# Attention projections as three float16 products of split rows and weights, split on ScalarE and GpSimd

## The chip, the cores and the metric

The kernel runs on one core of a Trainium2 chip. The metric is the device time of one execution in microseconds, and the time stated for a kernel is the median of its runs. One execution of each kernel is recorded by the hardware profiler. In the profile TensorE is PE (its weight loads are PEld), VectorE is DVE, ScalarE is ACT, GpSimd is POOL and SyncE is SP, whose queue starts the DMAs.

## What is computed

The input `x` is 2 x 128 x 256 x 256 (batch, channels, height, width) in float32. Two layers follow, each added to its own input: a window attention and a 3 x 3 convolution, each over a group norm of 32 groups.

```python
x = x + _L0_conv_ref(_gn(x), W_qkv, W_out, rel_height, rel_width)
x = x + _L1_conv_ref(_gn(x), weight, bias)
...
qkv = jnp.einsum('bchw,oc->bohw', x, W_qkv)
q, k, v = jnp.split(qkv, 3, axis=1)
q = q.reshape(b, INNER, nW, WS, nW, WS).transpose(0, 2, 4, 3, 5, 1)
k = unfold_windows(k)
v = unfold_windows(v)
...
attn = jnp.einsum('bnd,bmd->bnm', q * SCALE, k)
attn = attn + rel_pos_emb(q, rel_height, rel_width) + FIXED_MASK
attn = jax.nn.softmax(attn, axis=-1)
out = jnp.einsum('bnm,bmd->bnd', attn, v)
...
return jnp.einsum('bchw,oc->bohw', out, W_out)
```

Windows are 8 x 8 positions for the queries and 12 x 12 for keys and values (two rows and columns of halo), with 4 heads of 32 channels. The mask lets a query see only those keys whose row and column have one parity each, so the work falls into four parts by the parity of row and column. All products of the attention have 128 channels or fewer on the contracted side.

## The kernel before

The program runs in three stages, one after the other. The first reads `x` once for the group norm's moments (`bn_stats`) and prepares the weights. The second, the attention, is the subject here. The third is the convolution, which has already its rows and weights split into a high and a low float16 part and computes three products (`th` by `wc_h`, `tl` by `wc_h`, `th` by `wc_l`).

**Units and groups.** The attention handles 128 units. A unit is a strip of 8 rows by 128 columns (half a row of the image; `h` is the half), with its halo. A unit has 16 windows, four groups `g` of four windows each, and its rows are kept by parity in `PAR = 4` planes of `PLANE = 396` columns (66 x 6). Group number `n = 4u + g`. Every engine has its own program, written out by hand as `body(u, s, slot, on)`, which is called for each unit `u` and contains all that the engine does in the time of that unit for several units at different depths of the pipeline; a loop of four such bodies runs over the middle units. The engines meet through counting semaphores (`need` and `wait_ge`). So the order within an engine is fixed by the text of its `body`, and an instruction that waits holds up all that stand behind it on that engine.

**TensorE** (lines 378 to 468), in each group: the scores of group n (`ps_s`, 16 products, L421), the first transposes of group n-3 (`ps_t`, L401), `project` (L386 the query product of 256 columns into `ps_q`, L389 the key product of 396 columns into `ps_k`) of one of the next unit's four pieces, the value products of group n-3 (L434: for each of the four planes, 108 columns of `zf` are the loaded operand and 128 columns of `wq` are streamed), the products with the probabilities of group n-4 (`ps_o`, L451), the second transposes of n-3 (L401), and the output product (L462), which shares the bank `ps_q` with the query product. A float32 product is two matmul instructions in the trace.

**VectorE** (lines 471 to 552): adds the output product to `x1` (L495), sums the relative logits (L502 to `brel`), sums the exponentials (L506), copies the relative logits out (L511), reciprocal (L517), adds `erel` to the scores (L521), and takes their maximum (L527). To this come, in g0, two `bn_stats` (L533), in g1 and g3 the four copies from `qf` into the block-diagonal `qb` (L541), and in g2 two reductions over tiles (L548). The scores of a unit's g0 wait for both `qb` copies of that unit.

**ScalarE** (lines 555 to 622): exponential of n-2 (L576), the copy of the first transposes to `pt` (L581), of the query (L562) and key (L566) products, of the values (L588), of the output of the heads (L593), of the second transposes (L599), and then a piece of the normalised rows `zf` of unit u+2: in g0 a one-column copy that carries a wait (L608) and the rows of one parity (L610), in g1 those of the other, in g2 the two halo rows (L616).

**GpSimd** (lines 625 to 662): `erel` (L635), the normalised probabilities `d` (L642), two products for the relative logits (L651), and the subtraction of the maximum (L658).

**SP** (lines 347 to 376): loads the rows `xb` of unit u+3, stores `x1`, and loads the rows that are added to it.

`zf` has four slots of four planes, `xb` two halves. `z_at` addresses a plane of a slot.

## Time and profile before

| | |
|---|---|
| Time, median of 3 runs | 4083.1 us (4082.2 to 4085.4) |
| The profiled execution | 4085.44 us, with a span of 4083.6 us |
| Matmuls (PE) busy | 3730.3 us, 91% of the span |
| VectorE (DVE) busy | 3414.0 us, 84% |
| ScalarE (ACT) busy | 2976.6 us, 73% |
| GpSimd (POOL) busy | 2257.8 us, 55% |
| Chain that ended last | `ps_c` L808, 25% of the span, which is the convolution stage |

The span runs from the first to the last instruction of the execution, and what lies around it is about 1.8 us. The page cuts the span into forty slices, and these show three parts: the first stage up to about 200 us, in which TensorE does nothing, the attention up to about 3020 us, and the convolution from about 3060 us to the end. In the attention every slice looks like the one before. A busy share is the share of time in which a record of the engine is open; consecutive records of one engine overlap by some 0.1 us, so that the distance from start to start is the better measure of what an instruction costs its engine, and from start to end of what it costs who waits for it. The chain of the page follows only what ended last, and since the stages are separated it stops at the convolution; the attention has to be read from its timeline and its waits.

### The profile page before, as it was taken

The numbers are of one execution on the slowest core, as the hardware profiler recorded it, in microseconds if no ns is written. First come the engines' busy times: TensorE is split into PE (matmuls) and PEld (weight loads), VectorE is DVE, ScalarE is ACT, GpSimd is POOL, SyncE is SP. The second block draws the span as 40 slices with busy tenths as digits, with TensorE's granted clock in tenths as the row PEclk, the third lists the DMA queues.
The fourth block names the chain that finished last, engine by engine and source line by source line (L and its number), as shares of the span: only waits on it lengthen the run. The fifth ranks groups of instructions, "written<-read, shape, count | busy, mean of one in ns | idle before, by whom it ended". The sixth has DMA issues, their size and how long they took to land. (4 is left out here: it accounts for less than half of the span.)

```text
span 4083.6 us, 130797 instructions
## 1 busy us (share of the span) xinstructions
PE 3730.3 (91%) x48644; PEld 2631.8 (64%) x48644; DVE 3414.0 (84%) x6126; ACT 2976.6 (73%) x5317; POOL 2257.8 (55%) x2824
## 2 busy tenths in 40 slices
PE   0089999999999999999999999999958999999999
PEld 0067777777777777777777777777743444444444
DVE  9868888888888888888888888888878888888887
ACT  0078778778778878878877878877737777777774
POOL 0045555555555555555555555555536666666664
PEclk9999999999999999999999999999979999999999
DMA  9723233333233233233233233233214333343332
GB/s 372 312 75 86 82 93 85 83 93 86 81 93 87 81 93 87 80 93 87 80 93 88 79 93 87 80 93 87 73 58 173 152 149 152 149 153 152 155 145 94
DMA packets 489933, 462.48 MB, mean 113 GB/s; under 512 B 9264, under 2 KB 468912, under 8 KB 469040
## 3 DMA queue, kind: packets, MB, share of 16 engines
q1 hardware_dynamic: 489520, 455.92, 34.6%
q8 instruction: 388, 6.36, 0.6%
q14 instruction: 25, 0.20, 0.0%
HBM read 321.40 MB, written 134.48 MB: 112 GB/s over the span
## 5 line engine op out<-in xcount | busy, mean ns | idle before, releaser
L635 POOL TENSOR_TENSOR sb_erel<-sb_brel 128x288 f32<-128x288 f32 x512 | 352.1, 688 | 871.3 <-DVE sb_brel L502 871.2
L900 POOL TENSOR_TENSOR sb_tf<-sb_cf 128x1024 f32<-128x1024 f32 x256 | 609.6, 2383 | 393.1 <-DVE sb_tl L882 371.1
L651 POOL TENSOR_TENSOR sb_prod<-sb_rel,sb_shift 128x192 f32<-128x192 f32 x1024 | 596.8, 603 | 199.8 <-DVE sb_rel L511 199.8
L421 PEld LDWEIGHTS ps_s<-sb_kf,sb_qb 128*64 128x64 f32 x16384 | 520.3, 138 | 254.7 <-issue 237.0
L401 PE MATMUL ps_t<-sb_ident,sb_d 128*108 128x128 f32 x4096 | 662.4, 284 | 1.0 <-ACT sb_pt L599 1.0
L541 DVE COPY sb_qb<-sb_qf 32x512 f32<-32x512 f32 x1024 | 635.8, 621 | 27.6 <-ACT sb_qf L562 16.3
L421 PE MATMUL ps_s<-sb_kf,sb_qb 128*64 128x54 f32 x16384 | 586.3, 225 | 76.3 <-DVE sb_qb L541 73.8
L808 PE MATMUL ps_c<-sb_th,sb_wc_h 128*128 128x512 f16 x1536 | 584.9, 381 | 39.9 <-DVE sb_tl L882 39.9
L434 PEld LDWEIGHTS ps_v<-sb_wq,sb_zf 128*108 128x108 f32 x4096 | 511.1, 173 | 153.0 <-issue 80.5
L808 PE MATMUL ps_c<-sb_th,sb_wc_l 128*128 128x512 f16 x1536 | 583.9, 380 | 0.0
L808 PE MATMUL ps_c<-sb_tl,sb_wc_h 128*128 128x512 f16 x1536 | 583.8, 380 | 0.0
L434 PE MATMUL ps_v<-sb_wq,sb_zf 128*108 128x128 f32 x4096 | 530.4, 272 | 0.0
L642 POOL TENSOR_TENSOR sb_d<-sb_scores,sb_srcp 128x288 f32<-128x288 f32 x512 | 343.4, 671 | 282.6 <-DVE sb_srcp L517 269.4
L581 ACT COPY sb_pt<-ps_t 108x512 f32<-108x512 f32 x512 | 298.2, 582 | 226.1 <-PE ps_t L401 226.1
L401 PEld LDWEIGHTS ps_t<-sb_ident,sb_d 128*108 128x108 f32 x4096 | 410.7, 131 | 79.2 <-issue 2.1
L835 ACT CAST sb_th<-sb_tf 128x1024 f16<-128x1024 f32 x256 | 264.0, 1043 | 259.9 <-POOL sb_tf L900 257.9
L389 PE MATMUL ps_k<-sb_zf,sb_wq 128*128 128x396 f32 x1024 | 424.9, 496 | 0.0
L882 DVE TENSOR_TENSOR sb_tl<-sb_tf,sb_th 128x1024 f16<-128x1024 f32 x256 | 406.8, 1589 | 20.4 <-ACT sb_th L835 20.3
L495 DVE SCALAR_TENSOR_TENSOR sb_x<-ps_q,sb_oscale,sb_x 128x256 f32<-128x256 f32 x512 | 247.4, 483 | 202.7 <-PE ps_q L462 194.5
L566 ACT COPY sb_kf<-ps_k 128x576 f32<-128x576 f32 x512 | 329.6, 644 | 110.2 <-PE ps_k L389 97.4
L872 DVE SCALAR_TENSOR_TENSOR sb_oc<-ps_c,sb_wscale,sb_oc 128x1024 f32<-128x1024 f32 x256 | 322.6, 1281 | 95.5 <-PE ps_c L808 95.5
L506 DVE TENSOR_REDUCE sb_ssum<-sb_scores 128x8 f32<-128x288 f32 x512 | 230.6, 450 | 204.7 <-ACT sb_scores L576 191.5
(96 smaller groups left out, 6703.0 us busy)
## 6 DMA issues: line engine op xcount, KB each, us to landing
sb_xb<-rows SPq DMA_DIRECT2D x128, 780.0 KB, 6.7
sb_xc<-x SPq DMA_DIRECT2D x64, 1280.0 KB, 5.4
sb_abuf<-rows SPq DMA_DIRECT2D x32, 2048.0 KB, 10.8
sb_x<-rows SPq DMA_DIRECT2D x128, 512.0 KB, 3.9
x<-sb_x SPq DMA_DIRECT2D x128, 512.0 KB, 3.9
out<-sb_oc SPq DMA_DIRECT2D x64, 1024.0 KB, 3.8
sb_raw<-wconv SPq DMA_DIRECT2D x1, 576.0 KB, 4.0
x<-sb_zrow SPq DMA_DIRECT2D x2, 128.0 KB, 2.1
```

The source lines that it names most:

```text
L389: pe.matmul(ps_k[:, 0:PLANE], wq[:, C:2 * C], z_at(slot, p, 0, [[1, PLANE]]), start=True, stop=True).then_inc(sem["k_mm"], 1)
L401: last = pe.transpose(ps_t[0:KV, wj * 128:(wj + 1) * 128], d[:, at:at + KV], ident[:])
L421: last = pe.matmul(s_at, qb[:, qc:qc + QB], kf[:, kc:kc + KR], start=True, stop=True)
L434: last = pe.matmul(ps_v[0:KV, p * C:(p + 1) * C], z_at(vslot, p, GW * WK * vg, [[1, KV]]), wq[:, 2 * C:3 * C], start=True, stop=True)
L541: last = dve.tensor_copy(view(qb, DH * hd, DH * hd + DH, (1 - h) * QBW + p0 * NW * QB + hd * QN, [[QB, 2 * NW], [1, QN]]), view(qf, DH * h ...
L566: act.copy(view(kf, 0, 128, vh * KU + p * NW * KR, [[KR, NW], [1, KN]]), view(ps_k, 0, 128, 0, [[WK, NW], [1, KN]])).then_inc(sem["kf_done ...
L635: pool.tensor_tensor(view(erel, 0, 128, 0, [[KN, PAIRS], [KS, KS], [1, KS]]), view(brel, 0, 128, 0, [[KS, PAIRS], [0, KS], [1, KS]]), view ...
L642: pool.tensor_tensor(view(d, 0, 128, b0 * DB, [[DSLOT, PAIRS], [1, KN]]), view(sp_, 0, 128, b0 * NS, [[KN, PAIRS], [1, KN]]), view(srcp, 0 ...
L651: last = pool.tensor_tensor(view(prod, 0, 128, ax * PAIRS * KS * QS, [[KS * QS, PAIRS], [QS, KS], [1, QS]]), view(rel, 0, 128, b0 * PAIRS ...
L808: last = pe.matmul(m_at, wt[:, tap], t_at(z), start=(c == 0), stop=(c == 8))
L882: dve.tensor_tensor(view(tl, 0, 128, at, [[CW, PAIRROWS], [1, W]]), view(tf, 0, 128, k * TF, [[W, PAIRROWS], [1, W]]), view(th, 0, 128, at ...
L900: pool.tensor_tensor(tf[:, k * TF:(k + 1) * TF], view(cf, 0, 128, c0 + ra * W, [[2 * W, PAIRROWS], [1, W]]), view(cf, 0, 128, c0 + rb * W, ...
```

## The change

The three projections are computed from float16 parts. The weights `wq` become `wq_h` (rounded to float16) and `wq_l` (what is left), made once in the first stage. The normalised rows are still written to `zf` in float32 by ScalarE, and then split: ScalarE copies a plane to `zh` in float16 (`high`, one plane in each group) and GpSimd subtracts that from `zf` into `zl`, one plane in each group. Each float32 product becomes three float16 products, accumulated in the same place: `zh` by `wq_h`, `zh` by `wq_l`, `zl` by `wq_h`.

`zf` shrinks to two slots, as it is only the source of the split; `zh` and `zl` have four. The halo rows of a unit are written one group earlier in the order (in g3 of three units ahead, `edge_rows`, with the one-column copy), the other rows in g0 and g1 as before (`own_rows`); they now signal `zf_done` twice per unit. TensorE waits before each query product for its plane of `zl` (`zl_done`), where it waited once per unit for `zf_done`. The SP queue's load of `xb` waits for the new count of `zf_done`. The value products read `zh` and `zl` as the loaded operand.

```diff
                     dve.tensor_copy(wc_h[:], gw[:, 0:TAPS * C]).then_inc(w_hi, 1)
                     dve.tensor_copy(wo[:], rawn[:, SPANS[1][0]:SPANS[1][1]])
-                    dve.tensor_copy(wq[:], rawn[:, 0:3 * C])
+                    dve.tensor_copy(wq_h[:], rawn[:, 0:3 * C]).then_inc(w_hi, 1)
                     for b in range(2):
                         dve.tensor_copy(view(kf, 0, 128, b * KU + KN, [[KR, PAR * NW], [1, 2 * RN]]),
                                         view(rawn, 0, 128, 3 * C, [[0, PAR * NW], [1, 2 * RN]]))
-                    dve.wait_ge(w_hi, 1)
+                    dve.wait_ge(w_hi, 2)
+                    dve.tensor_tensor(wq_l[:], rawn[:, 0:3 * C], wq_h[:], ALU.subtract)
                     dve.tensor_tensor(wc_l[:], gw[:, 0:TAPS * C], wc_h[:], ALU.subtract)
                     with dve.bass.Fori(0, A_TILES // A_RING, engines=[dve.engine], hint_back_edge=True) as i:
                         for r in range(A_RING):
...
-                return view(zf, 0, 128, (slot % 4) * PAR * PLANE + p * PLANE + off, dims)
+            def z_at(z, slot, p, off, dims):
+
+                return view(z, 0, 128, (slot % 4) * PAR * PLANE + p * PLANE + off, dims)
+
+            PRODUCTS = ((zh, wq_h), (zh, wq_l), (zl, wq_h))
 
             block = pb.enter_context(nc.Block())
 
...
-                        need(sp, sem["zf_done"], u + 2)
+                        need(sp, sem["zf_done"], 2 * (u + 2))
...
-                    if p == 0:
-                        pe.wait_ge(sem["zf_done"], u + 1)
+                    pe.wait_ge(sem["zl_done"], piece + 1)
                     need(pe, sem["x1_done"], n - 2 * GROUPS)
                     need(pe, sem["qf_done"], piece)
-                    pe.matmul(ps_q[:, 0:QP], wq[:, 0:C], z_at(slot, p, KS + 1, [[KS, UW // 2], [1, QS]]),
-                              start=True, stop=True).then_inc(sem["q_mm"], 1)
+                    for c, (z, w) in enumerate(PRODUCTS):
+                        last = pe.matmul(ps_q[:, 0:QP], w[:, 0:C], z_at(z, slot, p, KS + 1, [[KS, UW // 2], [1, QS]]),
+                                         start=(c == 0), stop=(c == 2))
+                    last.then_inc(sem["q_mm"], 1)
                     need(pe, sem["kf_done"], piece)
-                    pe.matmul(ps_k[:, 0:PLANE], wq[:, C:2 * C], z_at(slot, p, 0, [[1, PLANE]]),
-                              start=True, stop=True).then_inc(sem["k_mm"], 1)
+                    for c, (z, w) in enumerate(PRODUCTS):
+                        last = pe.matmul(ps_k[:, 0:PLANE], w[:, C:2 * C], z_at(z, slot, p, 0, [[1, PLANE]]),
+                                         start=(c == 0), stop=(c == 2))
+                    last.then_inc(sem["k_mm"], 1)
 
                 def transposes(m, par, py):
...
-                                last = pe.matmul(ps_v[0:KV, p * C:(p + 1) * C],
-                                                 z_at(vslot, p, GW * WK * vg, [[1, KV]]),
-                                                 wq[:, 2 * C:3 * C], start=True, stop=True)
+                                for c, (z, w) in enumerate(PRODUCTS):
+                                    last = pe.matmul(ps_v[0:KV, p * C:(p + 1) * C],
+                                                     z_at(z, vslot, p, GW * WK * vg, [[1, KV]]),
+                                                     w[:, 2 * C:3 * C], start=(c == 0), stop=(c == 2))
                             last.then_inc(sem["v_mm"], 1)
                         if on(n - 4, GT):
...
-                        if g < 3 and on(u + 2, UNITS):
-                            s2_ = s + 1
-                            off = ((slot + 2) % 4) * PAR * PLANE + (1 - h) * KS
-                            col = lambda part: bass.ds(s2_ + part * STRIPS, 1)
-                            if g == 0:
-                                need(act, sem["v_mm"], (u - 1) * GROUPS)
-                                act.wait_ge(x_loaded[h], (s + 2) * 16)
-                                act.copy(aspare[:], bias[:])
-                            if g < 2:
-                                act.activation(
-                                    view(zf, 0, 128, off + 2 * g * PLANE + 1, [[PLANE, 2], [KS, LC // 2], [1, QS]]),
-                                    view(xb, 0, 128, (h * ZR + PAD + g) * LC, [[1, 2], [2, LC // 2], [2 * LC, QS]]),
-                                    ACT.Identity, bias=shift_t[:, col(1)], scale=rstd_t[:, col(1)])
-                            else:
-                                for part, row, ky in ((0, 0, 0), (2, ZR - PAD, KS - 1)):
-                                    last = act.activation(
-                                        view(zf, 0, 128, off + ky, [[2 * PLANE, 2], [PLANE, 2], [KS, LC // 2]]),
-                                        view(xb, 0, 128, (h * ZR + row) * LC, [[LC, 2], [1, 2], [2, LC // 2]]),
-                                        ACT.Identity, bias=shift_t[:, col(part)], scale=rstd_t[:, col(part)])
-                                last.then_inc(sem["zf_done"], 1)
+                        if g == 3 and on(u + 3, UNITS):
+                            edge_rows(u + 3, s + 1 + h, 1 - h)
+                        if g < 2 and on(u + 2, UNITS):
+                            own_rows(s + 1, h, g)
+                        split = u + 1 if g == 0 else u + 2
+                        if on(split, UNITS):
+                            high(split, slot if g else slot - 1, (g + 3) % PAR)
+
+                def column(strip, part):
+                    return bass.ds(strip + part * STRIPS, 1)
+
+                def edge_rows(v, strip, vh):
+
+                    need(act, sem["zl_done"], (v - 1) * PAR)
+                    act.wait_ge(x_loaded[vh], (strip + 1) * 16)
+                    act.copy(aspare[:], bias[:])
+                    off = vh * PAR * PLANE + (1 - vh) * KS
+                    for part, row, ky in ((0, 0, 0), (2, ZR - PAD, KS - 1)):
+                        act.activation(view(zf, 0, 128, off + ky, [[2 * PLANE, 2], [PLANE, 2], [KS, LC // 2]]),
+                                       view(xb, 0, 128, (vh * ZR + row) * LC, [[LC, 2], [1, 2], [2, LC // 2]]),
+                                       ACT.Identity, bias=shift_t[:, column(strip, part)],
+                                       scale=rstd_t[:, column(strip, part)])
+
+                def own_rows(strip, vh, py):
+
+                    off = vh * PAR * PLANE + (1 - vh) * KS
+                    act.activation(view(zf, 0, 128, off + 2 * py * PLANE + 1, [[PLANE, 2], [KS, LC // 2], [1, QS]]),
+                                   view(xb, 0, 128, (vh * ZR + PAD + py) * LC, [[1, 2], [2, LC // 2], [2 * LC, QS]]),
+                                   ACT.Identity, bias=shift_t[:, column(strip, 1)], scale=rstd_t[:, column(strip, 1)]
+                                   ).then_inc(sem["zf_done"], 1)
+
+                def high(v, vslot, p):
+
+                    if p == 0:
+                        need(act, sem["v_mm"], (v - 3) * GROUPS)
+                        act.wait_ge(sem["zf_done"], 2 * (v + 1))
+                    act.copy(z_at(zh, vslot + 2, p, 0, [[1, PLANE]]),
+                             view(zf, 0, 128, (vslot % 2) * PAR * PLANE + p * PLANE, [[1, PLANE]])
+                             ).then_inc(sem["zh_done"], 1)
                 act.wait_ge(sem["zeroed"], 1)
                 units(act, body)
...
+                        v, p, vslot = (u + 2, g - 2, slot + 2) if g >= 2 else (u + 1, g + 2, slot + 1)
+                        if on(v, UNITS):
+                            pool.wait_ge(sem["zh_done"], v * PAR + p + 1)
+                            pool.tensor_tensor(z_at(zl, vslot, p, 0, [[1, PLANE]]),
+                                               view(zf, 0, 128, (vslot % 2) * PAR * PLANE + p * PLANE, [[1, PLANE]]),
+                                               z_at(zh, vslot, p, 0, [[1, PLANE]]), ALU.subtract
+                                               ).then_inc(sem["zl_done"], 1)
```

## Rows read from the trace of the kernel before

**Rows 1.** Two windows of attention: length, busy time (instructions) per engine, PE clock, DMA.

```profile
core 0: us, PE busy (x) PEld busy (x) DVE busy (x) ACT busy (x) POOL busy (x), PEclk, DMA share, GB/s
1000.00:1400.00 400.00, 389.19 (x6288) 311.63 (x6287) 333.49 (x731) 320.55 (x605) 234.67 (x366) 1.00 0.31 87
2200.00:2600.00 400.00, 388.53 (x6281) 310.73 (x6280) 333.83 (x730) 318.88 (x602) 234.32 (x366) 1.00 0.32 88
```

**Rows 2.** Timeline of TensorE, one unit: start us, us, engine, line, operation, count.

```profile
1501.45 1.14 PE L421 MATMUL ps_s<-sb_kf,sb_qb 128*64 128x54 f32 x32 [0.53 <-DVE sb_qb L541]
...
1503.01 0.60 PE L386 MATMUL ps_q<-sb_zf,sb_wq 128*128 128x256 f32 x2
1503.45 0.83 PE L389 MATMUL ps_k<-sb_zf,sb_wq 128*128 128x396 f32 x2
1504.11 1.04 PE L434 MATMUL ps_v<-sb_wq,sb_zf 128*108 128x128 f32 x8
1505.08 0.65 PE L451 MATMUL ps_o<-sb_pt,sb_vf 108*32 108x64 f32 x32
1505.66 0.65 PE L401 MATMUL ps_t<-sb_ident,sb_d 128*108 128x128 f32 x4
...
1510.88 0.65 PE L401 MATMUL ps_t<-sb_ident,sb_d 128*108 128x128 f32 x4
...
1523.26 1.14 PE L421 MATMUL ps_s<-sb_kf,sb_qb 128*64 128x54 f32 x32 [0.52 <-DVE sb_qb L541]
```

**Rows 3.** Timeline of ScalarE, from g0 to g1 of that unit.

```profile
1506.35 0.59 ACT L599 COPY sb_pt<-ps_t 108x512 f32<-108x512 f32 x1 [0.17 <-PE ps_t L401]
1506.83 0.19 ACT L608 COPY sb_aspare<-sb_bias 128x1 f32<-128x1 f32 x1
1506.92 1.33 ACT L610 ACTIVATE sb_zf<-sb_xb,sb_shift_t,sb_rstd_t 128x520 f32<-128x520 f32 x1
1508.15 0.52 ACT L576 ACTIVATE sb_scores<-sb_scores,sb_alpha 128x288 f32<-128x288 f32 x1
```

**Rows 4.** Timeline of VectorE, the same unit.

```profile
1503.27 0.46 DVE L521 TENSOR_TENSOR sb_scores<-ps_s,sb_erel 128x288 f32<-128x288 f32 x1 [0.21 <-POOL sb_erel L635]
...
1508.70 0.45 DVE L506 TENSOR_REDUCE sb_ssum<-sb_scores 128x8 f32<-128x288 f32 x1 [0.97 <-ACT sb_scores L576]
...
1510.20 2.52 DVE L541 COPY sb_qb<-sb_qf 32x512 f32<-32x512 f32 x4
...
1513.16 0.54 DVE L502 TENSOR_REDUCE sb_brel<-sb_prod 128x96 f32<-128x384 f32 x1
1513.84 0.45 DVE L506 TENSOR_REDUCE sb_ssum<-sb_scores 128x8 f32<-128x288 f32 x1
...
1519.10 0.45 DVE L506 TENSOR_REDUCE sb_ssum<-sb_scores 128x8 f32<-128x288 f32 x1 [0.54 <-ACT sb_scores L576]
...
1520.60 2.52 DVE L541 COPY sb_qb<-sb_qf 32x512 f32<-32x512 f32 x4
```

**Rows 5.** Timeline of GpSimd, the same unit: g0, then g1.

```profile
1504.79 0.67 POOL L658 TENSOR_TENSOR sb_scores<-sb_scores,sb_smax 128x288 f32<-128x288 f32 x1
...
1511.60 0.85 POOL L658 TENSOR_TENSOR sb_scores<-sb_scores,sb_smax 128x288 f32<-128x288 f32 x1
```

**Rows 6.** Groups by shape, 3200 to 4000 us (convolution): busy us, mean ns, idle before.

```profile
L900 POOL TENSOR_TENSOR sb_tf<-sb_cf 128x1024 f32<-128x1024 f32 x206 | 486.8, 2363 | 315.6 <-DVE sb_tl L882 315.6
...
L835 ACT CAST sb_th<-sb_tf 128x1024 f16<-128x1024 f32 x206 | 212.5, 1044 | 216.1 <-POOL sb_tf L900 216.1
...
L808 PEld LDWEIGHTS ps_c<-sb_th,sb_wc_h 128*128 128x128 f16 x1232 | 120.3, 98 | 146.3
```

**Rows 7.** The chain that ended last, in order of time: start us, us, what.

```profile
3077.39 1000.62 PE ps_c L808 x4608
```

**Rows 8.** Weight loads by shape, 1000 to 2000 us (attention).

```profile
L421 PEld LDWEIGHTS ps_s<-sb_kf,sb_qb 128*64 128x64 f32 x5856 | 185.8, 138 | 88.2 <-issue 88.2
L434 PEld LDWEIGHTS ps_v<-sb_wq,sb_zf 128*108 128x108 f32 x1464 | 182.8, 173 | 55.6 <-issue 29.2
L401 PEld LDWEIGHTS ps_t<-sb_ident,sb_d 128*108 128x108 f32 x1468 | 147.2, 131 | 27.7
```

10 lines of the change are left out of this document (5 added, 5 removed).

## The prediction

> **What bounds the kernel now.** I began with busy time by stretch. The attention stage is steady, and in it TensorE is busy 97% of the time at the full granted clock, with VectorE and ScalarE at 83% and 80% [rows 1]. That looks like a kernel bound by TensorE, which the change relieves. The timeline of one unit (four groups g0 to g3, some 21.8 us) says something narrower. Between groups TensorE runs back to back at 5.22 us a group (the second transposes of g0 and of g1 start 5.22 us apart), but 4 x 5.22 is 20.88, and the unit takes 21.81 (the scores of g0 start at 1501.45 and at 1523.26). Before each unit's first scores TensorE stands idle for 0.52 us, for the last copies into `qb` [rows 2]. So I followed the ring that closes one unit, in four pieces:
>
> - TensorE, scores of g0 (1501.45) to the end of the second transposes of g0 (1505.66 + 0.65): 4.86 us [rows 2].
> - ScalarE, from there through the copy to `pt` (1506.35), the one-column copy (1506.83), the rows of `zf` (1506.92) and the exponential of g1, which ends at 1508.15 + 0.52: 2.36 us with the hand-over [rows 3].
> - VectorE, from the sum of g1 (1508.70) to the last `qb` copy of g3 (1520.60 + 2.52 = 1523.12): 14.42 us. It idles 0.14 us in g2 and 0.54 us in g3, both times for the exponential, so 13.74 is work [rows 4].
> - VectorE to TensorE and the small hand-over to VectorE: 0.17 us.
>
> They sum to 4.86 + 2.36 + 14.42 + 0.17 = 21.81. Only what changes one of these pieces changes the time. TensorE's share on it is g0 alone; in g1 to g3 VectorE carries the ring.
>
> **TensorE's new products.** In the convolution 4608 float16 products of 512 columns take 1000.62 us, 0.217 each [rows 7]: 0.213 for the columns at 2.4 GHz and 0.004 over. Now the query product goes from 0.44 us (1503.01 to 1503.45) and the key product from 0.66 (1503.45 to 1504.11) [rows 2] to 3 x (0.107 + 0.004) = 0.33 and 3 x (0.165 + 0.004) = 0.50. The saving is 0.11 and 0.16.
>
> The value products are the uncertain ones: 128 columns are streamed against 108 freshly loaded ones. Now there are 8 instructions in 0.97 us (1504.11 to 1505.08) [rows 2]. By the query's rate one streams for 0.11, so seven spacings make 0.76 and 0.21 is left for the last and the change to the next group. Afterwards there are 12. Streaming gives 0.053 + 0.004 = 0.057 each. Loading: a float32 load takes 138 ns for 64 columns and 173 for 108, which is 0.80 ns a column on a base of 87; but the transposes' float32 load of the same 108 columns takes 131 [rows 8], 0.41 a column, and the float16 load of 128 columns takes 98 [rows 6], 0.09 a column. A float16 load of 108 is in no row. Its ends are 0.09 and 0.80 ns a column; I take 0.41, because streaming float16 also goes at just half the float32 time, and half of 0.80 is 0.40. That is 43 ns, and with some 14 ns between a load and its product (an estimate from the score products: 16 pairs in the 1.14 us less 0.06 of overlap [rows 2] are 67 ns each, where a load of 64 needs 51 at 0.80) 57 ns, level with streaming. Eleven spacings of 0.057 and 0.15 for the end make 0.78, a saving of 0.19. At 0.09 it stays 0.78, since streaming binds; at 0.80 it is 11 x 0.100 + 0.18 = 1.28, a loss of 0.31.
>
> Here the Trainium skill speaks against the change. "TensorE: Matmul & The Clock Gate" (LDWEIGHTS) gives a load as its columns over 1.2 GHz, whatever the type, and its section on weight-path perf modes grants the fast load only to 128 columns that aren't float32. By that, 108 columns take 90 ns and the value products some 1.3 us. The trace agrees for float32 (0.80 a column) and for the fast load of 128; it disagrees for the transposes (131 ns), so I don't take the rule as settled. The same page's back-to-back figure for 128 columns, 81 ns a pair, would give an estimate of 1.05 us.
>
> TensorE's piece of the ring: 4.86 - 0.11 - 0.16 - 0.19 = 4.40. A group falls from 5.22 to 4.76.
>
> **ScalarE's split.** `high` casts 396 elements from SBUF. The convolution's cast of 1024 takes 1044 ns [rows 6] and the one-column copy starts its follower 0.09 us later [rows 3]. About 0.83 ns an element on 190 ns gives 0.52 us, of which 0.10 overlaps the next instruction (the copy to `pt` of 0.59 is followed after 0.48 [rows 3]): 0.43 us, once per group. Bounds are 0.36 and 0.60. One of them stands in g0 ahead of the exponential of g1: on the ring. The one-column copy leaves this place for g3 (0.09 off), and so does the pair of edge-row instructions, from g2 to g3. ScalarE's piece is 2.36 + 0.43 - 0.09 = 2.70. The edge rows now wait for the load of `xb` at g3, a group earlier than before. The SP queue can issue that load once VectorE's two tile reductions of the unit before are through, a unit ahead, and it isn't late. What is queued behind that wait is the whole evict order of ScalarE; if the load were late, each of its microseconds would count.
>
> **VectorE's piece.** No instruction is added to it. Its two waits for the exponential should go. In g2 the exponential comes one (shorter) group later; in g3 ScalarE has only a cast of 0.43 where the edge rows' 1.3 us stood. In their place VectorE runs up against GpSimd's `erel`, which costs 0.21 us where the sum doesn't wait (as at g0, 1503.27) [rows 4]. So 13.74 + 2 x 0.21 = 14.16. Bounds: 13.74 and 14.42.
>
> **GpSimd's split.** The subtraction takes two inputs of 396. Such an instruction takes 0.67 us for 288 elements [rows 5] and 2.36 for 1024 [rows 6]; 396 lies between 0.85 and 0.93. In g1 and g3 it runs beside the `qb` copies (1510.20 [rows 4]), where the same subtraction of scores takes 0.85 in place of 0.67 [rows 5], so there up to 1.2. A float16 output is in no row of this engine; bounds 0.7 and 1.7, I take 0.9 and 1.15. In g1 it would follow the score subtraction (ends at 1511.60 + 0.85 = 1512.45) and be ready at 1513.6, 4.9 us after VectorE's sum. TensorE, two shorter groups on, wants it in g2 some 3.9 us after that sum, so it will stand for about 1 us, **a new wait**, `ps_q` <- GpSimd, with the whole rest of g2 queued behind it. It costs nothing as long as TensorE then still reaches the next unit's scores before the `qb` copies end: 3.2 us of g2 and 4.8 of g3 are left and 9.1 remain, and the output product of g2 must be there before VectorE's reductions end, about 0.5 us of room. Beyond that the subtraction's excess counts in full. Below that, an excess still delays `erel`.
>
> **Sum.** 4.40 + 2.70 + 14.16 + 0.17 = 21.43 us a unit, 0.38 less. TensorE saves 0.46 a group, 1.84 a unit, and four fifths of it don't arrive. Of 128 units some 125 are steady: 47 us. The first unit waits for one more cast and one subtraction in a row (+1.5), the weight split adds two VectorE instructions in the prologue (+0.5). Sum 45 us less. The profiled execution took 4085.4 with a span of 4083.6, its runs' median is 4083.1, so 4083 - 45 = 4038.
>
> **Rivals.**
> - *Weight loads bind the value products* (slower). At the float32 rate they take 1.28: TensorE's piece is 4.90, a group 5.26, the exponential waits return (+0.3), the period is 22.2 and the time 4083 + 125 x 0.4 + 2, about 4135. For it: the float32 rows. Against: the transposes' load. It turns at some 85 ns a product (value products about 1.1 us), where the period is 21.8 again.
> - *A middle rate* (no change): value products about 1.05 us, period 21.75 to 21.85, 4075 to 4088.
> - *GpSimd becomes late* (slower): with a subtraction of 1.5 to 2.0 us the wait in g2 passes its room and `erel` slips, 0.1 to 0.6 us a unit over the forecast: 4050 to 4113. For it: GpSimd is already held up beside the `qb` copies. Against: it is idle for 40% of the stage [rows 1].
> - *VectorE isn't held by `erel`* or the cast is cheap (faster): the piece of 13.74, period 21.0, 3988; half of it, 4010.
> - *TensorE really is the bound* (the reading of the busy share): 4 x 0.46 a unit, 4083 - 230 = 3853. Against: the wait for `qb` at each unit's start, which a faster TensorE only lengthens. 2%.
>
> **Chances.** Forecast, 4018 to 4060: 0.50. Faster still: 0.10. No change: 0.13. Weight loads: 0.14. GpSimd late: 0.11, half of it still faster. TensorE the bound: 0.02. That makes faster 0.64, same 0.13, slower 0.23. Within 0.2% (8 us) is about what a measurement of this kernel can't tell from no change. The range 4003 to 4110 leaves out the slow weight loads and the far ends.
>
> **What would show it.** Spacing of the value products of 57 ns (right) or 90 to 104 (rival). A unit of 21.4 us. The idle time of TensorE before g0's scores, for `qb`, grown from 0.5 to about 1.2 us, and a new idle time of about 1 us before the query product of g2, for `zl`. No more VectorE idle time for the exponential in g3, but some for `erel`. A convolution stage of unchanged length. I would be wrong if ScalarE's cast came elsewhere than ahead of g1's exponential on the ring, or if the strided float16 reads of the query product ran below the contiguous ones.

## The result

| | Time, median | Ratio to the kernel before (95% interval) |
|---|---|---|
| Before | 4083.6 us (4082.2 to 4085.4, 4 runs) | |
| Changed | 4121.1 us (4118.2 to 4126.5, 4 runs) | 1.0092 (1.0080 to 1.0104) |

The changed kernel is slower by 0.9%, where 1.1% faster was forecast and the range ended at 4110. Its profiled execution has a span of 4124.6 us. TensorE did get less to do. The page's busy times over the whole span:

```profile
PE 3529.3 (86%) x51716; PEld 2490.0 (60%) x51716; DVE 3514.0 (85%) x6125; ACT 3175.2 (77%) x5829; POOL 2739.3 (66%) x3336
```

and two windows of the attention (columns as in [rows 1]):

```profile
1000.00:1400.00 400.00, 355.40 (x6700) 287.67 (x6697) 345.13 (x727) 346.39 (x674) 300.26 (x435) 1.00 0.31 86
2200.00:2600.00 400.00, 355.34 (x6707) 287.55 (x6705) 346.52 (x726) 345.60 (x672) 301.26 (x437) 1.00 0.30 86
```

TensorE's share fell from 97% to 89% of the window and VectorE's rose from 83% to 86%, with no instruction added to it in the attention. The convolution is as long as before: 1000.46 us in the chain, against [rows 7]. So the loss is in the attention, and its units show it. This is TensorE's timeline of one unit (it answers to [rows 2]; the query, key and value products now have three lines each, of which the first stand here):

```profile
1501.05 1.14 PE L428 MATMUL ps_s<-sb_kf,sb_qb 128*64 128x54 f32 x32 [1.67 <-DVE sb_qb L549]
...
1502.60 0.30 PE L390 MATMUL ps_q<-sb_zh,sb_wq_h 128*128 128x256 f16 x1
1502.74 0.30 PE L390 MATMUL ps_q<-sb_zh,sb_wq_l 128*128 128x256 f16 x1
...
1503.01 0.33 PE L395 MATMUL ps_k<-sb_zh,sb_wq_h 128*128 128x396 f16 x1
...
1503.51 0.22 PE L442 MATMUL ps_v<-sb_wq_h,sb_zh 128*108 128x128 f16 x1
1503.57 0.22 PE L442 MATMUL ps_v<-sb_wq_l,sb_zh 128*108 128x128 f16 x1
...
1504.38 0.65 PE L459 MATMUL ps_o<-sb_pt,sb_vf 108*32 108x64 f32 x32
1504.97 0.65 PE L408 MATMUL ps_t<-sb_ident,sb_d 128*108 128x128 f32 x4
...
1513.41 0.30 PE L390 MATMUL ps_q<-sb_zh,sb_wq_h 128*128 128x256 f16 x1 [0.89 <-POOL sb_zl L692]
...
1523.14 1.07 PE L428 MATMUL ps_s<-sb_kf,sb_qb 128*64 128x54 f32 x29 [1.56 <-DVE sb_qb L549]
```

A unit takes 22.09 us here (1501.05 to 1523.14), against 21.81 of the unit in [rows 2] and 21.43 forecast. Both waits that the prediction named are there: 0.89 us for `zl` in g2, and the wait for `qb` ahead of the scores has grown from 0.52 to about 1.6. The ring's next pieces, ScalarE's (as [rows 3]):

```profile
1505.65 0.59 ACT L607 COPY sb_pt<-ps_t 108x512 f32<-108x512 f32 x1
1506.13 1.34 ACT L635 ACTIVATE sb_zf<-sb_xb,sb_shift_t,sb_rstd_t 128x520 f32<-128x520 f32 x1
1507.37 0.51 ACT L645 CAST sb_zh<-sb_zf 128x396 f16<-128x396 f32 x1
1507.79 0.53 ACT L584 ACTIVATE sb_scores<-sb_scores,sb_alpha 128x288 f32<-128x288 f32 x1
```

and VectorE's (as [rows 4]), with the `qb` copies of g1 and of g3:

```profile
1508.35 0.45 DVE L514 TENSOR_REDUCE sb_ssum<-sb_scores 128x8 f32<-128x288 f32 x1 [1.32 <-ACT sb_scores L584]
...
1509.85 2.52 DVE L549 COPY sb_qb<-sb_qf 32x512 f32<-32x512 f32 x4
...
1518.12 0.44 DVE L514 TENSOR_REDUCE sb_ssum<-sb_scores 128x8 f32<-128x288 f32 x1
...
1519.86 3.14 DVE L549 COPY sb_qb<-sb_qf 32x512 f32<-32x512 f32 x4
```

The four pieces of the ring are then:

| Piece | Before | Forecast | Measured |
|---|---|---|---|
| TensorE, scores to second transposes of g0 | 4.86 | 4.40 | 4.57 |
| ScalarE, to the end of g1's exponential | 2.36 | 2.70 | 2.70 |
| VectorE, sum of g1 to last copy of g3 | 14.42 | 14.16 | 14.65 |
| Hand-overs | 0.17 | 0.17 | 0.17 |
| Unit | 21.81 | 21.43 | 22.09 |

Most of the miss stands in one line. The four copies of g3 take 3.14 us in place of 2.52, those of g1 still 2.52. (The unit shown has 0.11 us between the value products and the product with the probabilities that most units don't have: over the units of the loop the median of TensorE's piece is 4.46, and that of the unit 21.99.) Taken singly, the last copy of g3 is long:

```profile
1521.94 1.07 DVE L549 COPY sb_qb<-sb_qf 32x512 f32<-32x512 f32 x1
```

Beside them stands GpSimd (as [rows 5]), first in g1, then in g3:

```profile
1509.92 1.37 POOL L678 TENSOR_TENSOR sb_prod<-sb_rel,sb_shift 128x192 f32<-128x192 f32 x2
1511.24 0.85 POOL L685 TENSOR_TENSOR sb_scores<-sb_scores,sb_smax 128x288 f32<-128x288 f32 x1
1512.05 1.12 POOL L692 TENSOR_TENSOR sb_zl<-sb_zf,sb_zh 128x396 f16<-128x396 f32 x1
...
1519.67 1.16 POOL L678 TENSOR_TENSOR sb_prod<-sb_rel,sb_shift 128x192 f32<-128x192 f32 x2
1520.80 0.84 POOL L685 TENSOR_TENSOR sb_scores<-sb_scores,sb_smax 128x288 f32<-128x288 f32 x1
1521.61 1.11 POOL L692 TENSOR_TENSOR sb_zl<-sb_zf,sb_zh 128x396 f16<-128x396 f32 x1
```

In g1 the first copy (1509.85) starts ahead of the first product (1509.92), and the order is copy, product, copy, product, copy, score subtraction, copy, subtraction for `zl`. In g3 the first product (1519.67) is ahead of the first copy (1519.86), everything is shifted by one, and the fourth copy stands behind the `zl` subtraction, the longest instruction of GpSimd. Each copy that stands behind a GpSimd instruction ends 0.27 to 0.29 us after it: the last of g3 at 1523.01, the subtraction for `zl` at 1522.72. This was the theory to test ("theory P" below): copy and GpSimd instruction exclude each other, they alternate, and what a group costs hangs on who starts first.

The whole attention is longer by 40 us (from the first scores of the first unit to those of the last). The 116 units in the loop take 22.08 us on average against 21.86: 26 us. The other 14 come from the twelve units ahead of the loop and behind it, which are written out in straight line.

### The profile page after: what moved, and what is told of

Its sections match the earlier page's. It is cut to its first block and busy times, and to the rows that moved or that the text cites. A ratio compares the mean times of both kernels' runs of the same rounds, so it can differ in the third digit from the quotient of the medians.

```text
span 4124.6 us, 138477 instructions
## 1 busy us (share of the span) xinstructions
PE 3529.3 (86%) x51716; PEld 2490.0 (60%) x51716; DVE 3514.0 (85%) x6125; ACT 3175.2 (77%) x5829; POOL 2739.3 (66%) x3336
## 5 line engine op out<-in xcount | busy, mean ns | idle before, releaser
L549 DVE COPY sb_qb<-sb_qf 32x512 f32<-32x512 f32 x1024 | 720.8, 704 | 28.2 <-ACT sb_qf L570 17.7
L692 POOL TENSOR_TENSOR sb_zl<-sb_zf,sb_zh 128x396 f16<-128x396 f32 x512 | 526.7, 1029 | 192.2 <-ACT sb_zh L645 192.2
L678 POOL TENSOR_TENSOR sb_prod<-sb_rel,sb_shift 128x192 f32<-128x192 f32 x1024 | 572.5, 580 | 3.2 <-DVE sb_rel L519 3.2
L685 POOL TENSOR_TENSOR sb_scores<-sb_scores,sb_smax 128x288 f32<-128x288 f32 x512 | 388.2, 758 | 0.3
L861 ACT ACTIVATE sb_cf<-sb_xc,sb_dtab,sb_ctab 128x32 f32<-128x32 f32 (+2 forms) x768 | 357.2, 552 | 27.3 <-DMA sb_xc<-x 25.9
L442 PE MATMUL ps_v<-sb_wq_l,sb_zh 128*108 128x128 f16 x2048 | 371.5, 220 | 0.0
```

The costliest lines, as they stand in the source:

```text
L442: last = pe.matmul(ps_v[0:KV, p * C:(p + 1) * C], z_at(z, vslot, p, GW * WK * vg, [[1, KV]]), w[:, 2 * C:3 * C], start=(c == 0), stop=(c = ...
L549: last = dve.tensor_copy(view(qb, DH * hd, DH * hd + DH, (1 - h) * QBW + p0 * NW * QB + hd * QN, [[QB, 2 * NW], [1, QN]]), view(qf, DH * h ...
L678: last = pool.tensor_tensor(view(prod, 0, 128, ax * PAIRS * KS * QS, [[KS * QS, PAIRS], [QS, KS], [1, QS]]), view(rel, 0, 128, b0 * PAIRS ...
L685: pool.tensor_tensor(view(sp_, 0, 128, b1 * NS, [[KN, PAIRS], [1, KN]]), view(sp_, 0, 128, b1 * NS, [[KN, PAIRS], [1, KN]]), view(smax, 0, ...
L692: pool.tensor_tensor(z_at(zl, vslot, p, 0, [[1, PLANE]]), view(zf, 0, 128, (vslot % 2) * PAR * PLANE + p * PLANE, [[1, PLANE]]), z_at(zh, ...
L861: last = act.activation(view(cf, 0, 128, c0 + off, dims), view(xc, 0, 128, r + off, dims), ACT.Identity, bias=dtab[:, col], scale=ctab[:, ...
```

## The experiments

Each kernel was run in three rounds beside the kernel before. "A unit" is the average distance from one unit's first scores to the next, over some 85 to 94 units in the loop; low-clock units are those in which the record of TensorE's granted clock shows a stretch at 1.2 GHz in place of 2.4. The unit of the kernel before is 21.86 by the same measure. The kernels of e2, e3, e6 and e7 leave out or replace a part of the computation, as their expectations say, so that their times are those of experiments and not of usable kernels.

| Run | Time | Ratio (95% interval) | Unit | Copies g1, g3 |
|---|---|---|---|---|
| changed kernel | 4121.1 | 1.0092 (1.0080 to 1.0104) | 22.06 | 2.52, 3.14 |
| e1_low_first_g3 | 4045.1 | 0.9902 (0.9886 to 0.9919) | 21.52 | 2.52, 2.44 |
| e9_copies_first | 4046.0 | 0.9906 (0.9890 to 0.9923) | 21.55 | 2.52, 2.52 |
| e2_short_low | 4039.0 | 0.9888 (0.9872 to 0.9905) | 21.51 | 2.52, 2.58 |
| e8_subtract_in_before | 4098.7 | 1.0036 (1.0022 to 1.0050) | 21.88 | 2.53, 2.52 |
| e5_split_alone | 4187.2 | 1.0252 (1.0235 to 1.0269) | 22.62 | 2.52, 3.14 |
| e6_products_alone | 4028.2 | 0.9862 (0.9846 to 0.9879) | 21.45 | 2.52, 2.50 |
| e3_one_product | 4227.9 | 1.0354 (1.0337 to 1.0371) | 23.05 | 2.52, 3.14 |
| e7_query_contiguous | 4140.2 | 1.0145 (1.0128 to 1.0162) | 22.22 | 2.53, 3.14 |
| e4_exp_early | 3965.9 | 0.9710 (0.9694 to 0.9726) | 20.94 | 3.15, 2.50 |
| e4b_exp_early_alone | 4145.8 | 1.0151 (1.0134 to 1.0168) | 22.39 | 3.15, 3.14 |
| e10_exp_early_copies_first | 3899.6 | 0.9545 (0.9530 to 0.9561) | 20.39 | 2.52, 2.38 |
| e11_reordered_before | 4049.6 | 0.9915 (0.9899 to 0.9932) | 21.60 | 2.53, 2.50 |

### Who goes first on GpSimd and VectorE

The first experiment moves one instruction, in g3 alone (`low` is the subtraction for `zl`, put ahead of the sum `erel` there):

```diff
+                FIRST_LOW = (3,)
...
+                        if g in FIRST_LOW and on(v, UNITS):
+                            low(v, vslot, p)
                         if on(n - 1, GT):
...
+                        if g not in FIRST_LOW and on(v, UNITS):
+                            low(v, vslot, p)
```

> The changed kernel with one step moved: in g3 GpSimd takes its subtraction for zl ahead of erel, where it stood idle for 0.88 us, and no longer at the end of the group. Nothing is taken away. Theory P (port): in g3 the fourth qb copy takes 1.07 us because it stands behind the subtraction; with nothing behind the score subtraction it should take 0.40, the four copies 2.52 or less in place of 3.14, and the ring of one unit 22.09 - 0.63 = 21.46 us. Over 125 units that is 79 us less than the changed kernel's 4121: about 4042, near 0.990 of the kernel before. Rival G (GpSimd is simply too busy, and erel comes late): the subtraction now delays erel of g3 by some 0.05 to 0.1 us, so the time stays or grows: 4121 to 4135. Rival T (TensorE's slower query products hold the unit): no change, 4121.

4045, as theory P had it (4042), by moving one instruction per unit. VectorE's piece of the ring, from the sum of g1 to the last copy of g3, is back at 14.01 us (median over the units of the loop), where the changed kernel has 14.65. The second moves nothing and adds a wait:

```diff
                             pool.wait_ge(sem["rel_out"], n + 1)
                             need(pool, sem["b_done"], n)
+                            if g in (3,) and on(n - 1, GT):
+                                pool.wait_ge(sem["max_done"], n)
                             for ax in range(2):
```

> The changed kernel with a wait ADDED: in g3 GpSimd's first product for the relative logits also waits until VectorE has the maximum, so that the first qb copy goes ahead of it. Nothing is moved or taken away. Theory P: the four copies then alternate with product, product, score subtraction, and the subtraction for zl comes behind the fourth: 2.52 in place of 3.14, the unit 22.05 - 0.55 = 21.5 us, 4121 - 68 = about 4053, faster than the kernel before through one wait more. If the order doesn't matter, the wait costs its 0.1 to 0.2 us or nothing: 4121 to 4145.

4046: 75 us less through one wait more. VectorE and GpSimd in g3 of this kernel:

```profile
1246.08 2.53 DVE L549 COPY sb_qb<-sb_qf 32x512 f32<-32x512 f32 x4
...
1246.34 1.18 POOL L680 TENSOR_TENSOR sb_prod<-sb_rel,sb_shift 128x192 f32<-128x192 f32 x2 [0.40 <-DVE sb_smax L535]
1247.48 0.84 POOL L687 TENSOR_TENSOR sb_scores<-sb_scores,sb_smax 128x288 f32<-128x288 f32 x1
1248.29 1.13 POOL L694 TENSOR_TENSOR sb_zl<-sb_zf,sb_zh 128x396 f16<-128x396 f32 x1
```

The same instructions on both engines, the `zl` subtraction as long as before, and the copies back at 2.53. That excludes GpSimd's load as such (theory G) and TensorE's products (theory T). The third shortens the subtraction to a quarter (`LOWC` is `PLANE // 4`) and keeps the order:

```diff
-                            pool.tensor_tensor(z_at(zl, vslot, p, 0, [[1, PLANE]]),
-                                               view(zf, 0, 128, (vslot % 2) * PAR * PLANE + p * PLANE, [[1, PLANE]]),
-                                               z_at(zh, vslot, p, 0, [[1, PLANE]]), ALU.subtract
+                            pool.tensor_tensor(z_at(zl, vslot, p, 0, [[1, LOWC]]),
+                                               view(zf, 0, 128, (vslot % 2) * PAR * PLANE + p * PLANE, [[1, LOWC]]),
+                                               z_at(zh, vslot, p, 0, [[1, LOWC]]), ALU.subtract
```

> The changed kernel with GpSimd's subtraction for zl cut to 99 of 396 columns in every group (the low part of the other columns stays zero, so that part of the computation is left out); the order is kept. The subtraction falls from 0.93 to about 0.4 us. Theory P: the fourth qb copy of g3 still stands behind it, but for less: 1.07 - 0.5 = 0.5 to 0.6 us, the ring about 21.55, the time near 4054. Rival T: TensorE's part of g0 is unchanged, so 4121. Rival G: as P in the sum, but with VectorE's idle time for erel gone (2 x 0.1 us) and the fourth copy unchanged, some 4090.

4039, copies of g3 2.58, a unit of 21.5 as expected. The time is 15 us below the 4054 expected: 18 us of the gain lie in the straight-line units, which the expectation didn't count. The fourth puts the subtraction into the kernel before:

```diff
                                                ALU.subtract).then_inc(sem["sub_done"], 1)
+                            pool.tensor_tensor(xl[:], xf[:], xh[:], ALU.subtract)
```

> The kernel before, with one idle subtraction added on GpSimd at the end of each group: 396 columns, float32 minus float16 into float16, from and into tiles of its own, which nobody waits for. GpSimd's load is then that of the changed kernel; ScalarE and TensorE are untouched. Theory P (port, and who goes first): in the kernel before, VectorE's first qb copy starts ahead of GpSimd's first product in g3 as in g1, so the fourth copy is the last to be held up, by the score subtraction, and the added subtraction falls behind all four: 2.52 us as before, the unit 21.8, 4084 to 4090. Theory G (each GpSimd instruction beside the copies costs, whatever the order): 0.6 us a unit, 4160.

In the loop it does nothing: 21.88 us against 21.86. The 15 us that it costs in all (4099; 4084 to 4090 was expected, so this part missed) lie in the straight-line units, into which two stretches at 1.2 GHz fall as well, and these units show the race once more. VectorE and GpSimd, first in the loop, then in a unit behind it:

```profile
1268.15 2.52 DVE L545 COPY sb_qb<-sb_qf 32x512 f32<-32x512 f32 x4
...
1268.21 1.37 POOL L657 TENSOR_TENSOR sb_prod<-sb_rel,sb_shift 128x192 f32<-128x192 f32 x2
...
2910.60 3.31 DVE L545 COPY sb_qb<-sb_qf 32x512 f32<-32x512 f32 x4
...
2910.58 1.16 POOL L657 TENSOR_TENSOR sb_prod<-sb_rel,sb_shift 128x192 f32<-128x192 f32 x2
```

GpSimd starts 0.06 us behind the first copy in the one and 0.02 ahead of it in the other, with the same code but for the loop, and the copies take 2.52 or 3.31. Why it is earlier outside the loop wasn't tried. In the kernel before it is as early there, but with nothing behind the score subtraction that cost only 0.15 us (2.67 in place of 2.52). In the changed kernel the copies of such a unit mostly take 3.31 and 3.06 us, and three of the four such units with the full clock throughout take 22.6 us in place of 22.0. Its TensorE also has six stretches at 1.2 GHz in the twelve straight-line units, where the kernel before has one, and four units that hold one take 1.7 to 2.2 us more than in the kernel before. So the 14 us named above are only in part the copies'; an estimate from these lengths gives each of the two about half.

### What the parts are worth

The split without the products, with the single float32 products from a `zf` of four slots:

```diff
-            PRODUCTS = ((zh, wq_h), (zh, wq_l), (zl, wq_h))
+            PRODUCTS = ((zf, wq),)
```

> The split alone: ScalarE and GpSimd make zh and zl as in the changed kernel, but TensorE computes the single float32 products of the kernel before, from a zf of four slots. The output is whole. The ring: TensorE's piece back at 4.86 to 4.95 (+0.3 against the changed kernel's 4.57), ScalarE's 2.70, VectorE's 14.65 or some more, as the exponential comes later in g2: 22.4 to 22.7 us a unit. Against the kernel before that is +0.6 to +0.9, 75 to 110 us: 4160 to 4195. If instead TensorE has been bound all along, a group takes 5.22 again and the unit 21.8 or a little more: 4083 to 4100.

+103 us against the kernel before, a unit of 22.62 as the ring had it. Without the products the split costs 0.76 us a unit. By the medians of the ring's pieces 0.34 of it is ScalarE's (2.71 against 2.37: the cast, less the one-column copy) and 0.44 VectorE's (14.86 against 14.42: 0.62 of copies, less 0.18 of waiting that is gone). The reverse, the products from constant `zh` and `zl` without cast and subtraction:

```diff
-                    pe.wait_ge(sem["zl_done"], piece + 1)
+                    if p == 0:
+                        pe.wait_ge(sem["zf_done"], 2 * (u + 1))
...
-                        if on(split, UNITS):
-                            high(split, slot if g else slot - 1, (g + 3) % PAR)
```

> The products alone: TensorE computes the three float16 products from zh and zl that are filled once with constants; no cast and no subtraction is made for any unit (the split is left out, the output is not that of the input). ScalarE's piece of the ring is 2.27, TensorE's 4.5, VectorE's 14.16 or less, with no subtraction behind the copies: 21.0 us a unit, 4083 - 100 = about 3985. If the port theory is wrong and the fourth copy is long for another reason, VectorE's piece stays 14.65 and the unit takes 21.6, 4058.

4028, not 3985. The copies are back at 2.50, which is what the run was to decide, but 16 of 88 units have a stretch of TensorE at the low clock and take 22.6 us; the 72 others take 21.20 on average. That average hides two kinds of unit. Three in four take 20.93, a little under the 21.0 expected, with the ring's pieces at 4.46, 2.28 and 14.01. The unit of the last of the loop's four bodies takes 22.1 (median): TensorE idles 1.4 to 2.9 us there ahead of the next scores, in place of 1.16, and where that is long the profile names no instruction for which it waits ("issue"). The low clock falls only around that place, at the end of that unit or in the next. What holds TensorE there stays open. In e1, e9 and e10 the unit after that place is 0.3 to 0.5 us longer than the others, again with such waits. And one product in place of three:

```diff
-            PRODUCTS = ((zh, wq_h), (zh, wq_l), (zl, wq_h))
+            PRODUCTS = ((zh, wq_h),)
```

> The changed kernel with one float16 product (zh by wq_h) in place of three (the two small products are left out, the split is still made). TensorE has 1.0 us less to do in each group. If TensorE bound the stage, 4 x 1.0 us a unit would go, 500 us in all: 3620. By the ring only g0's group lies on it, and in g1 to g3 VectorE carries it: about 0.65 to 0.95 us a unit, 80 to 120 us: 4000 to 4040, with TensorE's idle time before the first scores grown to over 3 us.

Neither came. Two thirds of the projections' work were taken off TensorE, and the kernel became 107 us slower than the changed one. TensorE's waits in it from 1000 to 2000 us (idle us in total, times, longest), and the same stretch as a window, with its clock:

```profile
PE ps_s L428 <- DVE sb_qb L549: 121.4, 43, 3.1
PE ps_q L390 <- POOL sb_zl L692: 95.6, 77, 1.9
```

```profile
1000.00:2000.00 1000.00, 777.49 (x13888) 624.46 (x13886) 821.18 (x1740) 787.45 (x1611) 720.88 (x1046) 0.87 0.30 82
```

It idles 2.8 us ahead of each unit's scores (121.4 / 43), and the mean granted clock is 0.87 of full: every unit has a stretch at 1.2 GHz. VectorE's piece of the ring is 14.66 us as in the changed kernel, and TensorE's has grown from 4.46 to 5.39 (medians), although there is less in it. That it wasn't TensorE's work that bound the stage is plain; how much the ring alone would have given, this run can't say, for the clock came in between.

### TensorE's clock, and the query product's gaps

> The changed kernel with the query product reading 256 columns in a row in place of runs of four with gaps of two (the query values are then those of other positions, so that part is not the reference's). If the gaps in the float16 read cost the 0.137 us a product that the changed kernel shows, it falls to 0.111, the three take 0.33 in place of 0.41, and the unit is 0.08 us shorter: 4111. If the spacing of 0.137 has another cause, nothing changes: 0.137, 4121.

```diff
-                        z_at(z, slot, p, KS + 1, [[KS, UW // 2], [1, QS]])
+                        z_at(z, slot, p, KS, [[1, QP]])
```

The spacing fell from 0.137 to 0.109 us, as the first case said:

```profile
1504.58 0.27 PE L390 MATMUL ps_q<-sb_zh,sb_wq_h 128*128 128x256 f16 x1
1504.69 0.27 PE L390 MATMUL ps_q<-sb_zh,sb_wq_l 128*128 128x256 f16 x1
```

So the runs of four with gaps cost a float16 product 0.028 us of 0.137. (For float32 they cost little: 0.22 for 256 columns with gaps is 0.86 ns a column, and 0.33 for the key product's 396 without is 0.83, both from [rows 2].) But the time rose by 19 us instead of falling by 10. The 66 units without a low-clock stretch take 21.95, 0.10 less, as expected; 19 of 85 have one and take 23.2, where the changed kernel has it in 1 of 86. TensorE's idle time ahead of the scores had grown from 1.6 to 1.75 us, and with the faster products the clock fell more often.

The same appeared where only ScalarE's order was changed (the edit stands with e4_exp_early below, where e1's order on GpSimd is in the kernel too):

> The changed kernel with the exponential of g1 and g2 moved ahead as in e4_exp_early, but GpSimd's subtraction of g3 left at the end of the group. By the port theory the fourth copy of g3 keeps its 1.07 us and only the ring's ScalarE piece shortens: about 21.5 us a unit, near 4048. The difference to e4_exp_early should again be some 0.6 us a unit, 75 to 80 us.

4146 in place of 4048. The 37 units without a low-clock stretch take 21.53, which is the expectation; the 48 others take 23.05. TensorE's wait ahead of the scores over a stretch of 1000 us, then its timeline in one of the slow units, and windows of that unit:

```profile
PE ps_s L428 <- DVE sb_qb L549: 89.2, 45, 2.1
```

```profile
1282.93 1.14 PE L428 MATMUL ps_s<-sb_kf,sb_qb 128*64 128x54 f32 x32 [1.96 <-DVE sb_qb L549]
...
1284.69 0.42 PE L390 MATMUL ps_q<-sb_zh,sb_wq_h 128*128 128x256 f16 x1
```

```profile
1280.00:1284.00 4.00, 2.04 (x38) 1.58 (x39) 3.93 (x7) 3.17 (x7) 2.58 (x4) 1.00 0.84 236
1284.40:1287.40 3.00, 3.00 (x20) 2.23 (x19) 2.23 (x6) 1.58 (x3) 2.83 (x6) 0.50 0.62 180
1288.00:1300.00 12.00, 12.00 (x248) 9.65 (x238) 10.11 (x20) 11.54 (x23) 7.97 (x12) 1.00 0.01 1
```

The clock falls 1.3 us after the 1.96 us of idling have ended. It is at 0.50 (1.2 GHz) for 3.4 us, in which the query product takes 0.42 in place of 0.30, and then it is full again. Each such unit costs 1.5 us, and the earlier exponential, right by itself, had lengthened the idle time to 1.98 on average. In e1, e9 and e10, where the idle time is 0.9 to 1.0 us, and in e4 below, where it is 1.3, no unit of the loop is hit. But within one run the units that are hit have idled no longer than the others (1.73 us in e7 and 1.96 in e4b, medians of either kind), so that the idle time ahead of the scores alone doesn't tell which unit is hit.

### A version that is faster than both

The ring says what to do: the exponential of g1 needs neither the rows of `zf` nor the cast that ScalarE makes ahead of it. Moved ahead of them, with e1's order on GpSimd kept:

```diff
+                EARLY = (1, 2)
...
+                        if (g + 1) % GROUPS in EARLY and on(n - 1, GT):
+                            exponential(n - 1, b1)
                         if g == 3 and on(u + 3, UNITS):
                             edge_rows(u + 3, s + 1 + h, 1 - h)
                         if g < 2 and on(u + 2, UNITS):
                             own_rows(s + 1, h, g)
```

> The kernel of e1_low_first_g3 with the exponential of g1 and of g2 moved ahead on ScalarE: it is taken at the end of the group before, right after the copy to pt, ahead of the 1.24 us for the rows of zf and the 0.43 us of the cast. Nothing is taken away. By the ring ScalarE's piece falls from 2.70 to about 1.0 us; but then erel or the output product is next, so that not all of the 1.67 arrives: 20.7 to 21.0 us a unit, 4000 - 45 to 4000 - 10: about 3965. If the exponential isn't on the ring, the time stays that of e1_low_first_g3.

3965.9, as expected. But the race has now been lost in g1: the copies there take 3.15, since VectorE no longer waits for the exponential and comes after GpSimd. With the added wait of e9, for g1:

```diff
+                            if g in (1,) and on(n - 1, GT):
+                                pool.wait_ge(sem["max_done"], n)
```

> The kernel of e4_exp_early with the same added wait in g1: there VectorE no longer waits for the exponential, GpSimd's products went first, and the copies of g1 took 3.15. With the copies first they should take 2.52, and a unit 20.94 - 0.57 = 20.4 us: 3966 - 70 = about 3895, provided that TensorE's clock stays up; its idle time before the first scores should fall from about 1.4 to 0.8 us.

3899.6 us, 4.5% less than the kernel before and 5.4% less than the changed one, with TensorE busy again for 95% of the time:

```profile
1000.00:2000.00 1000.00, 952.79 (x18080) 779.64 (x18080) 893.23 (x1968) 915.28 (x1818) 797.39 (x1180) 1.00 0.33 93
```

The like in the kernel before (the exponentials of g1, g2 and g3 early, and the wait in g1):

```diff
+                EARLY = (1, 2, 3)
...
+                        if (g + 1) % GROUPS in EARLY and on(n - 1, GT):
+                            exponential(n - 1, b1)
...
+                            if g in (1,) and on(n - 1, GT):
+                                pool.wait_ge(sem["max_done"], n)
```

> The float32 kernel before with the same reordering as in e10_exp_early_copies_first: the exponential of g1, g2 and g3 moved ahead of the rows of zf on ScalarE, and GpSimd's products of g1 waiting for the maximum. It tells what the float16 products are worth once the order is right. With the exponential off the ring, TensorE is the bound here: four groups of 5.22 are 20.88, and the query product of g3 waits about 0.7 us for the halo rows of zf, 21.5 us a unit, 0.3 less: about 4043. Then the products and the split are worth 144 us against e10_exp_early_copies_first's 3900. If the reordering alone did it, this kernel would come to about 3900 too.

4049.6. The float32 kernel gains 34 us by the like reordering. There TensorE is the bound, busy for 979 of 1000 us, but for one wait a unit:

```profile
PE ps_q L386 <- ACT sb_zf L623: 21.2, 47, 0.5
```

That is 0.45 us each time, for the halo rows of `zf`, which the change writes a group earlier and this kernel doesn't. So the change, which cost 38 us as it was put in, is worth 150 us once the order is right. How much of this is the float16 products and how much the place of the halo rows was not tried. With that wait gone the float32 unit could at best fall from 21.60 to four groups of 5.22, 20.88. By this estimate up to 84 us over 116 units are the halo rows', and the products with their split are worth at least the other 66.

## Why the prediction was wrong

**The bound.** Right: the wait for `qb`, not TensorE's share, sets the unit, and ScalarE's and TensorE's pieces of the ring moved as worked out, within 0.01 and 0.06 us in most units. Four fifths of TensorE's saving were rightly written off; e1 (4045), in which the copies are no longer held up by the added subtraction, comes near the prediction's sum (4038).

**TensorE's products.** The key product is 0.50 (1503.01 to 1503.51), as forecast. The value products run at 0.056 each, against 0.057. The rival of slow weight loads falls: a float16 load of 108 columns takes 128 ns on the base of 87, 0.38 ns a column, near the 0.41 chosen:

```profile
L442 PEld LDWEIGHTS ps_v<-sb_wq_h,sb_zl 128*108 128x108 f16 x724 | 92.7, 128 | 0.0
```

That takes the base of the float32 loads for float16 too. The rule of the Trainium skill ("TensorE: Matmul & The Clock Gate", LDWEIGHTS) gives 90 ns for 108 columns; this case's trace disagrees, for the pairs follow each other after 56 ns. The 56 ns are also below the 81 of the same page's section on the back-to-back gap. The query product is the term that was mis-sized: 0.41 against 0.33, for its gaps (e7), which the prediction had named as a way to be wrong. The rest of the 0.17 in TensorE's piece is the 0.11 in the shown unit that most units don't have.

**ScalarE's cast.** Right within 0.01: 0.42 us from start to start, and the piece 2.70. The idle times of VectorE for the exponential in g2 and g3 are gone, as forecast.

**VectorE's piece.** Here is the step that failed: "No instruction is added to it", with bounds of 13.74 and 14.42. The measured 14.65 is above the upper bound. The prediction did see that GpSimd and the copies hold each other up, and used the row for that ([rows 5], 0.85 in place of 0.67), but only in one direction, to lengthen GpSimd's subtraction. The copies' side was in the same trace: [rows 4] gives 2.52 for four, and the first of them, which stands behind nothing, takes 0.41, so that the three others already waited for a GpSimd instruction. And it assumed that g3 keeps its order. In the kernel before the first copy led by only 0.06 us (1520.60 against 1520.66 here; GpSimd's `d` and first products in g3):

```profile
1520.04 0.67 POOL L642 TENSOR_TENSOR sb_d<-sb_scores,sb_srcp 128x288 f32<-128x288 f32 x1 [0.71 <-DVE sb_srcp L517]
1520.66 1.37 POOL L651 TENSOR_TENSOR sb_prod<-sb_rel,sb_shift 128x192 f32<-128x192 f32 x2
```

VectorE's wait for the exponential held back its reciprocal, and with it `d` and GpSimd's products. The same step that credited the vanishing wait (-0.26) removed what kept GpSimd behind. In the changed kernel both engines start from the end of `erel` (1518.28 + 0.69 = 1518.97):

```profile
1518.28 0.69 POOL L662 TENSOR_TENSOR sb_erel<-sb_brel 128x288 f32<-128x288 f32 x1 [0.88 <-DVE sb_brel L510]
1519.05 0.67 POOL L669 TENSOR_TENSOR sb_d<-sb_scores,sb_srcp 128x288 f32<-128x288 f32 x1
...
1519.00 0.46 DVE L529 TENSOR_TENSOR sb_scores<-ps_s,sb_erel 128x288 f32<-128x288 f32 x1
1519.49 0.45 DVE L535 TENSOR_REDUCE sb_smax<-sb_scores 128x8 f32<-128x288 f32 x1
```

GpSimd has only `d` ahead of its first product (1519.67), VectorE has the sum and the maximum ahead of its first copy (1519.86). This account of why the order turned is read from the two traces; that the order decides the copies' time is what e1 and e9 show. The price is 0.62 us a unit, 0.62 x 116 = 72 us; e1 and e9 got back 76 and 75.

The Trainium skill has a mechanism for this ("SBUF — State Buffer", Who interferes with whom): VectorE and GpSimd share a pair of ports under an exclusive lock, held for a whole instruction, which copies can take. The trace agrees with exclusion: the same copy takes 0.41 us alone, and 1.07 behind the subtraction for `zl`. In this trace the two engines alternate when both have work queued, so that a step of some 0.1 us in one start decides behind which instruction the last copy stands.

**The rivals.** "GpSimd becomes late" had the right engine and the wrong way: GpSimd was no later than forecast, for TensorE (a wait of 0.89 us for `zl`, off the ring) or for `erel`; it was early for VectorE. Its range (4050 to 4113) fell short too. TensorE as the bound is refuted by its idle time ahead of the scores, 1.59 us on average in place of 0.55, and by e3. The rival in which `erel` doesn't hold VectorE was near: without the 0.62 of copies VectorE's piece is 14.03, between its 13.74 and the forecast's 14.16.

**The rest.** The straight-line units (14 us) were taken as steady ones, and TensorE's clock was not in the sum. It is a small matter in the changed kernel: three of 116 units in the loop, and about half of the 14 us. But e4b and e7 show what it costs where TensorE's wait is a little longer.

## What to carry to other kernels

Where VectorE copies within SBUF on a critical ring, list GpSimd's instructions beside them in order, with the start of the first on either side: an instruction added to GpSimd costs VectorE nothing or most of its length (here 0.62 us for a subtraction of 0.94), depending on who leads, and one wait can settle it. A wait that a change removes may have been holding another engine back; ask who will now run ahead. And before making an engine faster that already waits, shorten the ring: the order of ScalarE's instructions was worth 80 us, and in e3 and e7 faster products with the ring left alone brought the clock down and the time up.

## What was not expected of the hardware

- VectorE's copy and GpSimd's instruction alternate strictly when both are queued: copies of 0.41 us alone take 0.64 behind a product, 0.80 behind a subtraction of 288 columns and 1.07 behind one of 396. GpSimd's instructions beside the copies are longer too: 0.85 in place of 0.67 us, and 1.12 in place of 0.94.
- TensorE's granted clock fell to 1.2 GHz for a stretch though the engine had idled no longer than 2.1 us at once in e7 and e4b. By the mean idle time ahead of the scores: 1 of 86 units was hit at 1.6 us, 19 of 85 at 1.75 (e7), 48 of 85 at 1.98 (e4b), and all 82 at 2.8 (e3, with waits for `zl` besides). Such units took 1.2 to 1.5 us longer in e7 and e4b. Within a run the units that were hit had not idled longer than the others; what decides was not tried.
- A float16 product that streams 256 columns in runs of four with gaps of two takes 0.137 us against 0.109 in a row.
